# Odd half of the forward row transform on twice folded samples

## What is computed

```python
# layer 0: 16x16 channel mix, leaky relu, scaled by minimum and maximum of each image and channel
# layer 1:
X = jnp.fft.rfftn(x, axes=(-2, -1), norm='backward')
Xr, Xi = jnp.real(X), jnp.imag(X)
Yr = _rconv(Xr, wr) - _rconv(Xi, wi) + b_real[:, None, None]     # 3x3, padded, over frequencies
Yi = _rconv(Xr, wi) + _rconv(Xi, wr) + b_imag[:, None, None]
return jnp.fft.irfftn(lax.complex(Yr, Yi), axes=(-2, -1), norm='backward')
# layer 2: 3x3 convolution of the input rounded to 8 bits; layer 3: 3x3 circular convolution
```

## Time and profile before

| | |
|---|---|
| Median of 3 runs | 6531.92 us (6527.77 to 6534.83) |
| Span of the profiled execution, its own time | 6537.8 us |
| Layer 1 stages: first to last odd transform of an image | about 383 us in seven images, 352 us in the last |
| Part with layers 2 and 3 | 4400 us to the end |

### The profile page before, as it was taken

The page is one execution under the profiler, slowest core; times in us unless marked ns, Lnnn a source line. Parts: engine busy times, 40 slices in busy tenths (PEclk is TensorE's granted clock), DMA queues, the critical chain, the costliest instruction groups (busy, mean ns, idle before and its releaser), DMA issues. The chain is left out here.

```text
span 6537.8 us, 200097 instructions
## 1 busy us (share of the span) xinstructions
PE 5657.3 (87%) x63882; PEld 3655.6 (56%) x63882; DVE 4850.6 (74%) x9636; ACT 4524.3 (69%) x8793; POOL 2728.2 (42%) x4634
## 2 busy tenths in 40 slices
PE   0289979979979989988988997995988989889889
PEld 0057748748747757756766775872433434334334
DVE  5778877877887887887887887767766667667664
ACT  2577767767766766767766556657877877778776
POOL 3165555656656556546646556650111111111112
PEclk9899989989999999999999999998999999999999
DMA  6516616615624633642651551553766767667665
GB/s 199 154 57 186 184 42 189 184 58 174 184 84 145 184 116 115 185 144 87 185 166 49 142 141 36 157 151 74 205 164 168 194 168 198 166 166 201 161 163 138
DMA packets 535620, 959.14 MB, mean 147 GB/s; under 512 B 121946, under 2 KB 126682, under 8 KB 532826
## 3 DMA queue, kind: packets, MB, share of 16 engines
q1 hardware_dynamic: 467546, 799.21, 44.2%
q10 hardware_dynamic: 67456, 151.01, 7.3%
HBM read 560.66 MB, written 287.60 MB: 130 GB/s over the span
## 5 line engine op out<-in xcount | busy, mean ns | idle before, releaser
L1635 PE MATMUL pC<-xs,taps 128*128 128x512 f16 x4608 | 1094.6, 382 | 107.7 <-DMA xhalo<-xs 100.6
L964 PE MATMUL pM<-gw,xh 64*128 64x256 f16 (+1 forms) x24960 | 1128.2, 244 | 0.0
L964 PEld LDWEIGHTS pM<-gw,xh 64*128 64x128 f16 x24960 | 966.8, 95 | 129.2 <-issue 3.3
L726 POOL TENSOR_TENSOR X<-X,zo 128x256 f32 (+1 forms) x512 | 371.2, 725 | 1218.1 <-DVE X L1084 1218.1
L1635 PEld LDWEIGHTS pC<-xs,taps 128*128 128x128 f16 x4608 | 448.7, 98 | 670.8 <-DVE xs L1685 89.9
L1531 POOL TENSOR_TENSOR xn<-xn,one_col 128x1 f32<-128x1 f32 x520 | 172.3, 331 | 1409.7 <-ACT xn L1565 1409.7
L1551 ACT ACTIVATE scaled<-X,qbias,qscale 128x512 f32 (+1 forms) x512 | 411.4, 804 | 335.4 <-DMA X<-after_layer 306.0
L272 PE MATMUL pM<-X,mix0s 64*64 64x512 f32 x2304 | 523.3, 624 | 136.7 <-DVE X L1056 108.6
L1084 DVE SCALAR_TENSOR_TENSOR X<-pZ,X 128x512 f32 (+1 forms) x512 | 354.1, 692 | 340.8 <-ACT zo L785 339.6
L1573 ACT ACTIVATE xs<-xn 128x1028 f16<-128x1028 f32 x520 | 545.7, 1049 | 87.5 <-POOL xn L1532 86.5
L711 POOL TENSOR_TENSOR X<-X,rl 128x512 f32 x384 | 478.3, 1276 | 267.5 <-ACT rl L756 267.3
(11 more groups left out here) (241 smaller groups left out, 13574.5 us busy)
## 6 DMA issues: line engine op xcount, KB each, us to landing
gw<-row_weights SPq DMA_DIRECT2D x520, 288.0 KB, 3.3
after_layer<-X SPq DMA_DIRECT2D x512, 256.0 KB
out_dram<-result SPq DMA_DIRECT2D x512, 256.0 KB
X<-in_x_dram SPq DMA_DIRECT2D x448, 256.0 KB
X<-after_layer ACTq DMA_DIRECT2D x224, 512.0 KB, 5.9
stage<-in_x_dram SPq DMA_DIRECT2D x192, 512.0 KB
xhalo<-xs SPq DMA_DIRECT2D x504, 96.4 KB, 3.6
qhalo<-q SPq DMA_DIRECT2D x496, 96.2 KB, 4.0
```

The lines of the kernel that those rows point to most:

```text
L726: nc.gpsimd.tensor_tensor(X[:, j, 0], X[:, j, 0], zo[:, k], ALU.add)
L964: nc.tensor.matmul(pY[:, r, col:col + nd * P], row(xh, r)[:, k, p, ri, off:off + P], weights(r, q_, d, nd, ri), start=ri == 0 and off == 1 ...
L1635: nc.tensor.matmul(bank, taps3[:, d, wh], xs[:, h, own, d:d + W], start=d == 0 and n == 0, stop=False)
```

## The change

The difference d[n] = x[n] - x[n+256] now goes to a tile `dif` of its own (257 wide, the last element zero). Because cos(2 pi n k/512) for odd k changes its sign under n -> 256-n and the sine keeps it, the cosine sums need only d[n] - d[256-n] and the sine sums only d[n+1] + d[255-n], 128 samples each. GpSimd makes both with a second operand that is read backward. PE then multiplies the first block with 128 cosines and the second with 128 sines. There are still six matmuls, each with 128 columns in place of 256. The halves of pF are written to the same places as before.

```diff
--- before.py
+++ after.py
@@ -83,7 +83,11 @@
     t["fwd_0"] = fwd(4 * np.arange(NO // 2 + 1), P)
     t["fwd_2"] = fwd(4 * np.arange(NO // 2 + 1) + 2, P)
     t["fwd_2"][..., NO // 2::NO // 2 + 1] = 0
-    t["fwd_odd"] = fwd(2 * np.arange(NO) + 1, HALF)
+    n, k = np.arange(NO)[:, None], 2 * np.arange(NO)[None, :] + 1
+    m = np.stack([np.cos(2 * np.pi * ((n * k) % W) / W),
+                  -np.sin(2 * np.pi * (((n + 1) * k) % W) / W) * np.where(n + 1 == NO, 0.5, 1.0)], 1) * F_SCALE
+    m[np.abs(m) < 1e-9] = 0
+    t["fwd_odd"] = np.stack(halves(m), 2)
 
     n2 = np.arange(HALF)
 
@@ -195,7 +199,7 @@
             bias0 = sb("bias0", [P, 1], f32, p1)
             fwd_0 = sb("fwd_0", [P, 1, 2, NO + 2], f16, p1)
             fwd_2 = sb("fwd_2", [P, 1, 2, NO + 2], f16, p1)
-            fwd_odd = sb("fwd_odd", [P, 2, 2, 2 * NO], f16, p1)
+            fwd_odd = sb("fwd_odd", [P, 2, 2, NO], f16, p1)
             inv_even = sb("inv_even", [P, 2, 2, HALF], f16, p1)
             inv_odd = sb("inv_odd", [P, 2, 2, HALF], f16, p1)
             biasrow = sb("biasrow", [P, W], f32, p1)
@@ -571,6 +575,7 @@
                 xh = sb("xh", [P, 2, 2, 2, XH + 1], f16, pm)
                 yt = sb("yt", [P, 2, 2, 4 * P], f16, pm)
                 even = sb("even", [P, 2, HALF], f32, pm)
+                dif = sb("dif", [P, HALF + 1], f32, pm)
                 stats_1 = even[:, 0, 0:3 * J].rearrange("p (g k s) -> p g k s", k=2, s=6)
                 zo = sb("zo", [P, 2, HALF], f32, pm)
                 es = zo[:, :].rearrange("p k w -> p (k w)")
@@ -600,7 +605,7 @@
                 yt_done, yt_hi, yt_lo = s_("yt_done"), s_("yt_hi"), s_("yt_lo")
                 zo_ready, x2_ready, sq2_done = s_("zo_ready"), s_("x2_ready"), s_("sq2_done")
                 z_done, z_free, edge_hi, edge_ready = s_("z_done"), s_("z_free"), s_("edge_hi"), s_("edge_ready")
-                even_done = s_("even_done")
+                even_done, dif_done, dif_free = s_("even_done"), s_("dif_done"), s_("dif_free")
                 tile_stats = s_("tile_stats")
                 pads_ready = s_("pads_ready")
                 SMALL = 7
@@ -698,8 +703,10 @@
 
                 @block.gpsimd
                 def _(pool):
+                    nc.gpsimd.memset(dif[:, HALF:HALF + 1], 0.0)
                     nc.gpsimd.memset(xh[:, :, :, :, :], 0.0).then_inc(pads_ready, 1)
                     pool.wait_ge(pads_ready, 1)
+                    pool.sem_inc(dif_free, 1)
 
                     def root(b, n):
                         pool.wait_ge(var_ready, b * 3 + n + 1)
@@ -712,8 +719,12 @@
 
                     def folded(b, i, k):
                         pool.wait_ge(xn_ready, b * ITEMS + i + 1)
+                        pool.wait_ge(dif_free, b * ITEMS + i + 1)
+                        nc.gpsimd.tensor_tensor(dif[:, 0:HALF], xn[:, k, 0:HALF], xn[:, k, HALF:W], ALU.subtract).then_inc(dif_done, 1)
                         nc.gpsimd.tensor_tensor(even[:, k], xn[:, k, 0:HALF], xn[:, k, HALF:W], ALU.add).then_inc(even_done, 1)
-                        nc.gpsimd.tensor_tensor(fold[:, k, HALF:W], xn[:, k, 0:HALF], xn[:, k, HALF:W], ALU.subtract)
+                        pool.wait_ge(dif_done, b * ITEMS + i + 1)
+                        nc.gpsimd.tensor_tensor(fold[:, k, HALF:HALF + NO], dif[:, 0:NO], dif[:, HALF:NO:-1], ALU.subtract)
+                        nc.gpsimd.tensor_tensor(fold[:, k, HALF + NO:W], dif[:, 1:NO + 1], dif[:, HALF - 1:NO - 1:-1], ALU.add).then_inc(dif_free, 1)
                         pool.wait_ge(even_done, b * ITEMS + i + 1)
                         nc.gpsimd.tensor_tensor(fold[:, k, 0:P], even[:, k, 0:P], even[:, k, P:HALF], ALU.add)
                         nc.gpsimd.tensor_tensor(fold[:, k, P:HALF], even[:, k, 0:P], even[:, k, P:HALF],
@@ -935,7 +946,7 @@
                                 pe.wait_ge(xh_lo, q + i - 1)
 
                             for n in range(2):
-                                three(pF[:, 0, 0:2 * NO], lambda h, c=n + 2: xt[:, o, h, c * P:(c + 1) * P],
+                                three(pF[:, 0, n * NO:(n + 1) * NO], lambda h, c=n + 2: xt[:, o, h, c * P:(c + 1) * P],
                                       lambda h, n=n: fwd_odd[:, n, h], n == 0, n == 1)
                             three(pF[:, 1, 0:NO + 2], lambda h: xt[:, o, h, 0:P], lambda h: fwd_0[:, 0, h], True, False)
                             m = three(pF[:, 1, NO + 2:2 * NO + 4], lambda h: xt[:, o, h, P:2 * P], lambda h: fwd_2[:, 0, h], False, True)
```

## The result

The changed kernel takes 6378.09 us (median of 4 runs, 6372.0 to 6390.0) against 6530.18 us before: ratio 0.9768, 95% interval 0.9751 to 0.9785, some 152 us less. The forecast was 6378.

A forecast was written before the change was run, and what follows sets the result against it. PE was taken to bound the stage: 62 items of an image save 0.31 us, 19.2 us, times 8 images 154 us, starts 0. From 6537.8 that gives 6384, for the median 6378 us; range 6366 to 6416.

The forecast's parts named there:

- PE sets the pace: Layer 1 stage: the other engines wait in a chain beginning at PE, so a step shortens by what PE saves.
- 0.31 us for an item: Six fwd_odd matmuls start 0.058 us apart, not 0.109; 62 items of each of 8 images save 0.31 us, 154 us.
- Reserves: Steady steps: after the change ACT has 1.33 us left, DVE 0.82, GpSimd 1.19 on average with a turn of 4.60.
- the handover of yt: Tightest handover found, DVE's L1121 to the next convolution, which overwrites pY: 1.44 us before, 0.82 left after.
- Backward reading: GpSimd's 128-wide operations with a backward operand take 0.46 us as forward; rival at 0.90 us each: 6411 us, chance 0.10.
- The bound of 0.90: Upper price in us for a 128-wide backward GpSimd operation, from the dearest such run before; kept for the range.
- Start of an image, up to the first convolution: Three folds take 0.92 us more each, second odd transform 0.9 late, half-clock savings offset it; net taken as 0.
- The wait for edge_back: At an image's start PE waits 0.54 us at 955.85; one further transform's saving in front of it is waited.
- the clock rising later: Image start: clock rises one group later, 2 us each, 16 in all, 6394 us; chance 0.07.
- The slower rival: GpSimd becomes the bound if a backward operation exceeds 1.18 us; at 1.35 some 235 us more, 6767; chance 0.03.
- The weight load as the limit: fwd_odd matmuls: the 98 ns load isn't hidden at 128 columns; an item saves 6 x 11 ns, 6499 us; chance 0.03.
- the Trainium skill's rule of 81 ns: Sustained load and matmul pairs at 128 columns take about 81 ns: an item saves 0.17 us, near 6449 us; not used.

The follow-up runs named there:

- after: The profiled execution of the changed kernel itself, nothing further changed; the changed kernel's median is 6378.09 us, ratio 0.9768 to the kernel before.
- again: The changed kernel itself run once more, nothing changed, as the measure for two later runs on the same chip: 6378.91 us, ratio 0.977.
- dve_even: Changed kernel, with the sum even of the first two items of an image made by DVE in place of GpSimd: 6380.07 us, ratio 0.9763.
- warm: Changed kernel, with twelve 128x512 matmuls on constant tables run by TensorE ahead of an image's first fold: 6380.88 us, ratio 0.9762.

## Why the prediction was right, point by point

- **PE sets the pace.** Right. Both halves undone give it: without the narrow matmuls the rest is 2915.5 us, without the new folds 2762.4.
- **0.31 us for an item.** The distance is 56 ns, not 58, so 0.32. The rest of the eight stages fell by 152.9 us, where the 60 items that count there make 148.8 at 0.31 and 153.6 at 0.32.
- **Reserves.** ACT 1.32 us (1.33 said), DVE 0.81 (0.82), the handover of yt 1603.55 to 1604.35 = 0.80 (0.82). GpSimd's turn 1604.88 to 1609.32 = 4.44 us (4.60 said; successive operations overlap by some 0.04 us each), its wait 1.34 (1.19).
- **Backward reading.** 459 ns against 456 forward: free, the value I took. The bound of 0.90 was also met, beside DVE at the edge item (one in each image, 902 ns on L726 and up to 906 on L727), as forward operations met 0.90 before. So it comes from DVE's work beside it and not from the direction.
- **Start of an image, up to the first convolution.** The forecast was no change: it began 927.93 - 916.44 = 11.49 us after the first fold, where 11.51 stood before and 11.5 was said. The second odd transform came 10.08 us after the first fold in place of 9.46, 0.62 late (0.9 said), and was 0.64 shorter at the half clock.
- **Start of an image, behind it.** The wait for edge_back took the saving of one item, 0.86 us instead of 0.54, as said. Two things were missed. The third odd transform's saving was counted in the 62 items, but the wait for yt at the second convolution takes it, 8 x 0.31 = 2.5 us; the handover of yt was looked at in the steady part alone. And what I put in a rival with a chance of 0.07, the clock rising later, came in part: the eight first convolutions took 2.99 to 3.32 us before, and now 3.0 in three images, 3.3 in one and 3.7 to 3.8 in four, 2.4 us more in all. The starts grew by 2.2 us where they should have fallen by 2.5. Some 2.2 of the 16 us of that rival are real, 0.3 for an image.
- **The hit.** The starts cost 4.7 us more than forecast and the rest gained 4.1 us more. That the median comes out 0.1 us from the forecast is luck: these two errors cancel, and the four runs spread over 18 us. The size of the gain, 152 us of 154 forecast, isn't luck, since the stage table has it in the steady part.
- **The slower rival.** Its bound was right in kind: it decides where a turn is longer than the step. At +0.6 us a turn little but the starts moved, at +1.8 the kernel became slower than before. Its sum for b = 1.35 has a wrong term: by its own prices the starts would cost 3 x 1.78 x 8 = 43 us and not 21, some 6789 us in place of 6767.
- **The weight load as the limit** (and the Trainium skill's rule of 81 ns beside it). Not so here: 56 ns in the changed kernel, 29 at 64 columns.

What stays open: how the instant at which the clock rises depends on the start; I only saw that it differs between images of one execution (second to third transform 5.19 to 5.95 us in the changed kernel), and that filling the gaps removes it. The other variation between runs of one kernel, 18 us in the changed kernel's four and 42 in seventeen of before, lies outside these stages as far as two traces show it: the spans of `after` and `again`, the same kernel, differ by 11.1 us, their stages by 0.6. What varies there is open too.

## What to carry to other kernels

Where an engine's list is dense, price its work by the distance of starts of the nearest like stream, and give each other engine a reserve: its wait per step in the trace. A transfer of work from the bound engine to an idle one is free up to that reserve in the steady part, but in the fill of a pipeline it lies on the path, once for every fill. Matmuls against a symmetric table can be halved by folding the samples ahead of it, as long as the folding engine's turn stays below the new, shorter step.

## What was not expected of the hardware

- A backward float32 operand costs GpSimd next to nothing: 459 against 456 ns (medians) for 128 elements, 520 times each. DVE's work beside it costs more: 902 ns in place of 459 at the edge item, 0.96 us in place of 0.73 for 256 elements in dve_even.
- Six loads of 128x128, each 98 ns long, with their matmuls of 64 columns went by in 0.17 us.
- The granted clock fell from 1.00 to 0.50 after 2.75 us of dense matmuls and 4.5 us of idleness; it was at half when it was needed (warm, second image). Matmuls whose result nobody reads, in the gaps themselves, kept it at 1.00.
